# A gated delta recurrence with one head-shared kernel on one core: leaf solutions computed in contiguous rows and copied back by ScalarE

## The reference

```python
def step(S, t):
    q_t, k_t, v_t, a_t, b_t = t
    y = jnp.einsum('bhvk,bhk->bhv', S, k_t)
    err = y - v_t
    S = a_t[..., None] * S - (b_t[..., None] * err)[..., None] * k_t[:, :, None, :]
    o = jnp.einsum('bhvk,bhk->bhv', S, q_t)
    return (S, o)
```

## Time and profile before

| what | value |
|---|---|
| three runs | 3316.79, 3305.04, 3324.02 us; median 3316.79 |
| the profiled execution | 3323.35 us, its span 3321.6 us |
| mean granted TensorE clock | 0.968 |
| PE, PEld busy | 2941.5 us (89%), 2047.0 us (62%) |
| DVE busy | 2412.1 us (73%) |
| ACT, POOL busy | 1604.8 us (48%), 1287.5 us (39%) |

### The profile page before, as it was taken

How to read it: one execution, slowest core, us unless ns; L and a number is a source line. 1 busy time by engine, 2 the same in 40 slices (tenths; PEclk the granted TensorE clock), 3 DMA queues, 4 the chain that set the end, 5 groups by cost and what they waited for, 6 DMA issues and landing times. The chain is left out here.

```text
span 3321.6 us, 47953 instructions
## 1 busy us (share of the span) xinstructions
PE 2941.5 (89%) x14232; PEld 2047.0 (62%) x14232; DVE 2412.1 (73%) x4820; ACT 1604.8 (48%) x3480; POOL 1287.5 (39%) x1455
## 2 busy tenths in 40 slices
...
DMA packets 429785, 253.02 MB, mean 76 GB/s; under 512 B 400016, under 2 KB 412016, under 8 KB 414832
## 3 DMA queue, kind: packets, MB, share of 16 engines
...
## 5 line engine op out<-in xcount | busy, mean ns | idle before, releaser
L245 DVE SCALAR_TENSOR_TENSOR A_acc<-A_psY,A_w,A_acc 128x410 f32<-128x410 f32 (+1 forms) x720 | 419.3, 637 | 156.0 <-ACT A_acc L285 156.0
L771 POOL TENSOR_TENSOR B_WT<-B_WT,B_G 128x128 f32<-128x128 f32 (+2 forms) x224 | 191.4, 854 | 779.2 <-issue 448.8
L1072 ACT ACTIVATE B_WL<-B_psT 128x128 f32<-128x128 f32 (+2 forms) x480 | 150.0, 313 | 530.6 <-PE B_psT L1489 530.6
L345 PE MATMUL A_psY<-A_xT,A_w 128*128 128x413 f32 (+1 forms) x960 | 347.2, 510 | 9.0 <-PE A_psAG L351 7.7
L202 POOL TENSOR_TENSOR A_outs<-A_outs,A_acc 128x410 f32<-128x410 f32 (+1 forms) x240 | 229.2, 986 | 254.0 <-ACT A_outs L293 254.0
L345 PEld LDWEIGHTS A_psY<-A_xT,A_w 128*128 128x128 f32 x960 | 180.2, 189 | 165.5 <-issue 164.2
L986 DVE TENSOR_TENSOR B_NC<-B_NC,B_psM 128x256 f32<-128x256 f32 x480 | 198.8, 414 | 113.6 <-PE B_psM L1516 94.7
L989 DVE TENSOR_REDUCE B_W<-B_NC 128x64 f32<-128x320 f32 x512 | 248.8, 486 | 17.6
L1516 PE MATMUL B_psM<-B_BD,B_WL 128*128 128x128 f32 x1536 | 238.1, 297 | 9.1
L285 ACT ACTIVATE A_acc<-A_psY,A_w 128x410 f32<-128x410 f32 (+1 forms) x240 | 166.0, 692 | 163.1 <-PE A_psY L345 161.5
L1516 PEld LDWEIGHTS B_psM<-B_BD,B_WL 128*128 128x128 f32 x1536 | 196.7, 198 | 75.4 <-ACT B_WL L1072 74.7
...
## 6 DMA issues: line engine op xcount, KB each, us to landing
...
```

Of the source, the lines that this page charges most:

```text
L245: nc.vector.scalar_tensor_tensor(a, y, w[:, s, col:col + 1], a, ALU.mult, ALU.add)\
L345: last = nc.tensor.matmul(psY[p][:, y0:y0 + HALO + t1 - t0], wp[:, p, kt, :], xT[:, kt, t0:t1 + HALO], start=kt == 0, stop=kt == KT - 1)
L771: tt(dst, dst, gr, ALU.mult).then_inc(wsc.sem, 1)
L1072: copy = lambda out, in_: nc.scalar.activation(out, in_, ACT.Copy)
```

## The change

The solution is now worked out in `WTOK` (8 rows of 128 contiguous elements, otherwise used only between the end of a chunk's leaves and its state update), in `TMP` with its dimensions exchanged, and in `X`; ScalarE's new `solution_copy(i, n)`, n = 0, 1, 2, copies the finished coefficient rows to `NC`. L986 of leaves 0 and 8 waits for the last of these copies (`ncc`, 3) in place of the eighth step. `leaf_diagonals` has nine copies in place of five. The eight steps keep their number, their element counts and their place. One of the two state decays of leaf 10 moves to leaf 11, behind `row_pairs`. On TensorE the last job of leaf 14 waits for L986 of leaf 15, and the two copies into `WTOK` at the end of a chunk wait for `ncc` of the next chunk's first half.

```diff
-        TMP = sb("TMP", [128, HJ2, 4])
+        TMP = sb("TMP", [128, 4, HJ2])
...
-        gb, nc0 = Count(sem("block_decays"), 3), Count(sem("leaf_diagonals"), 5)
+        gb, nc0 = Count(sem("block_decays"), 3), Count(sem("leaf_diagonals"), 9)
...
-        ncs = Count(sem("leaf_solutions"), NCS)
+        ncs, ncc = Count(sem("leaf_solutions"), NCS), Count(sem("leaf_solutions_copied"), 3)
...
                 ps = rows(take_bank(dve, g if h else g - 1, "kk", h, 0))
-                tt(n[:, :, :, :, 11], ps[:, 1], a[:, 1], ALU.mult).then_inc(nl.sem, 1)
-                tt(n[:, :, :, :, 16], ps[:, 2], rr, ALU.mult).then_inc(nl.sem, 1)
+                wait(dve, ncc, i, 0)
+                tt(as_rows(WTOK[:])[:, 4], ps[:, 1], a[:, 1], ALU.mult).then_inc(nl.sem, 1)
+                tt(as_rows(WTOK[:])[:, 1], ps[:, 2], rr, ALU.mult).then_inc(nl.sem, 1)
...
-                step(1, 0, TMP[:, :, 0:3], n[:, :, 6:17:5], many(n[:, :, 0:1], 3), ALU.mult)
-                step(2, 0, n[:, :, 12:18:5], x02, many(n[:, :, 7:8], 2), ALU.mult)
-                step(3, 1, n[:, :, 5:16:5], n[:, :, 5:16:5], TMP[:, :, 0:3], ALU.add)
-                step(4, 0, n[:, :, 18:19], x2, n[:, :, 13:14], ALU.mult)
-                step(5, 3, tmp2, many(x02.unsqueeze(3), 2, 2), many(n[:, :, 5:7].unsqueeze(2), 2, 2), ALU.mult)
+                step(1, 0, TMP[:, 0:3], S[:, 1:8:3], many(TMP[:, 3:4], 3), ALU.mult)
+                step(2, 0, S[:, 2:6:3], x02, many(S[:, 5:6], 2), ALU.mult)
+                step(3, 1, S[:, 0:7:3], S[:, 0:7:3], TMP[:, 0:3], ALU.add)
+                step(4, 0, n[:, :, 18], X[:, 2], n[:, :, 13], ALU.mult)
+                step(5, 3, tmp2, many(x02.unsqueeze(2), 2, 2), many(S[:, 6:8].unsqueeze(1), 2, 2), ALU.mult)
                 step(6, 5, rows23, rows23, tmp2, ALU.add)
-                step(7, 6, TMP[:, :, 0:3], many(x2, 3), n[:, :, 10:13], ALU.mult)
-                step(8, 7, n[:, :, 15:18], n[:, :, 15:18], TMP[:, :, 0:3], ALU.add)
+                step(7, 6, TMP[:, 0:3], many(x2, 3), S[:, 3:6], ALU.mult)
+                step(8, 7, S[:, 0:3], S[:, 0:3], TMP[:, 0:3], ALU.add)
...
                     if j == 0 or j == 8:
-                        wait(dve, ncs, 2 * g + h, NCS)
+                        wait(dve, ncc, 2 * g + h, 3)
...
                         decay_state(g, 0)
-                        decay_state(g, 1)
                     elif j == 11 and more:
                         row_pairs(nxt)
+                        decay_state(g, 1)
                         leaf_solution(nxt, 1, 2)
...
                 for l in range(2):
                     copy(n[:, l, :, :, 7::6], f[:, l]).then_inc(nc0.sem, 1)
-                    copy(n[:, l, :, :, 0::5], v[:, l]).then_inc(nc0.sem, 1)
+                copy(n[:, :, :, :, 0], v[:, 0]).then_inc(nc0.sem, 1)
+                S = as_rows(WTOK[:])
+                if i:
+                    wait(act, stu, (i - 1) // 2, 0)
+                wait(act, ncs, i, 0)
+                wait(act, ncc, i, 0)
+                for k in range(3):
+                    copy(S[:, 6 - 3 * k], v[:, 1 + k]).then_inc(nc0.sem, 1)
+                copy(as_rows(TMP[:])[:, 3], v[:, 0]).then_inc(nc0.sem, 1)
+                copy(S[:, 5], f[:, :, :, :, 0]).then_inc(nc0.sem, 1)
+
+            def solution_copy(i, n):
+
+                flat = NC[:, i % 2].rearrange("p l h n c -> p c (l h n)")
+                wait(act, ncs, i, (3, 6, 8)[n])
+                w_ = 3 if n else 2
+                copy(flat[:, 5 * n + 5:5 * n + 5 + w_], WTOK[:, 6 - 3 * n:6 - 3 * n + w_]).then_inc(ncc.sem, 1)
...
                     elif j == 7 and more:
+                        solution_copy(2 * g + 1, 1)
+                        solution_copy(2 * g + 1, 2)
                         decay_copies(g + 1)
                         leaf_keys(2 * g + 2)
...
+                    elif j == 13 and more:
+                        solution_copy(2 * g + 2, 0)
                     elif j == 14:
                         if more:
+                            solution_copy(2 * g + 2, 1)
                             block_keys(2 * g + 2)
+                    elif j == 15 and more:
+                        solution_copy(2 * g + 2, 2)
...
                     for job in leaf_jobs(g, j):
+                        if j == 14 and job == leaf_jobs(g, j)[-1]:
+                            wait(pe, ap, g, J)
```

More of the change, by code:

```diff
@@ L643, in _ @@
                 if g + 1 < NCH:
-                    wait(sp, nc0, 2 * g + 1, 5)
+                    wait(sp, nc0, 2 * g + 1, 9)
                     load("C0", n, at)
@@ L828, in decays @@
                 wait(dve, gb, g - 2, 1)
-                wait(dve, nc0, 2 * g - 3, 5)
+                wait(dve, nc0, 2 * g - 3, 9)
                 a, e = by_leaf_row(A[:, s]), E[:, s]
@@ L1027, in chunk @@
                         decay_state(g, 0)
-                        decay_state(g, 1)
                     elif j == 11 and more:
                         row_pairs(nxt)
+                        decay_state(g, 1)
                         leaf_solution(nxt, 1, 2)
+                    elif j == 11:
+                        decay_state(g, 1)
                     elif j == 12 and more:
```

31 lines of the change are left out of this document (21 added, 10 removed).

## The result

The changed kernel takes 3334.72 us (median of 20 runs, 3326.55 to 3339.71); the kernel before, in 20 runs beside it, 3322.61 us (3305.04 to 3331.77). The medians lie 12.1 us apart. The ratio is 1.0041, 95% interval 1.0029 to 1.0054: slower by 13.6 us, where +33 was forecast. The direction held, the size did not. That 3334.72 stands inside the forecast's own range, 3333 to 3367, is luck: the kernel before came out at 3322.61 in these runs, 5.8 us above the 3316.79 that the forecast was added to. The profiled execution spans 3332.8 us (before 3321.6) at a mean granted clock of 0.967 (0.968).

A forecast was written before the change was run, and what follows sets the result against it. TensorE and VectorE were near full, VectorE deciding from leaf 6 to 8, with ScalarE's copies put behind it. Terms 20 + 12 - 10 + 11 = +33 us, carried to the median 3316.79, gave 3350 us; range 3333 to 3367, chance 0.50.

The forecast's parts named there:

- VectorE's prices: Solution steps: 384 contiguous elements take 546 ns, saving 1.8 us a solution, 115 us of VectorE's time in 64 solutions.
- ScalarE's price: Solution copies into NC: 384 elements at the 80-byte pitch take 0.90 us, between 0.50 and 1.05.
- The rival that ScalarE decides nothing: Copies run at contiguous pace, 384 in 0.50 us: -16 us, 3301, chance 0.12; 3275 if step 7 escapes GpSimd, 0.08.
- Leaf 7 to 8: L986 of leaf 8 waits for ScalarE's solution copy: loss 0.70 us (bounds: gain 0.5, loss 0.95).
- The rival that L771 misses step 7: At leaf 7 GpSimd's instruction misses step 7: leaf 8 costs -0.10 us, leaf 9 0; +3 us, 3320, chance 0.13.
- Leaf 4 to 7: Leaf 6 starts 0.45 us later behind leaf_diagonals' nine copies; steps 1 to 3 then gain 0.68 from leaf 6 to 7.
- T6 comes 0.45 us later: T6 is the start of L986 of leaf 6; nine ScalarE copies delay it 0.45 us (bounds 0 and 0.8).
- Leaf 8 to 9: ScalarE's queue behind the solution copies ends later than L947's start: loss 0.15 us (0 to 0.4).
- Leaf 10 to 12: The moved decay's 0.60 us is lost again and 0.64 more, in 19 chunks at full clock: +12 us.
- Leaf 12 to 15: Shorter steps gain 0.2 us at leaf 12 in 19 chunks, 0.4 at leaves 13 and 14 in 16: -10 us.
- Chunk's end: Last solution copy ahead of the WE copy costs 0.67 us in 16 even chunks, +11 us; odd ones covered.
- The clock rival: TensorE's clock, fallen to 0.50 about leaf 11 in 13 of 32 chunks, falls in all: +54 us, 3371, chance 0.17.

The follow-up runs named there:

- experiment 7: Changed kernel with solution copies of 2 in place of 128 elements a row, most of the solution not reaching NC; ratio to the kernel before 0.9978.
- experiment 5: Changed kernel with GpSimd's L771 after leaf 7 on 128 of its 512 elements; ratio to the kernel before 1.0004, leaf 7 to 8 from 5.99 to 5.26 us.
- Experiment 4: Kernel before with four more 128-element ScalarE copies in leaf_diagonals, into WTOK, which nobody reads; ratio to the kernel before 1.0095.
- experiment 6: Kernel before with one state decay moved from leaf 10 to 11, ratio 1.0021; changed kernel with that decay put back, 1.0067.
- experiment 9: Changed kernel, four edits: step 8 into NC at leaf 7, last copy late, TensorE's wait out, value copies earlier: 1.001; with leaf 9's decay transposes doubled 0.9905.
- experiments 2 and 3: Changed kernel with the chunk's last solution copy behind the WE copy, ratio 1.0048; the same without TensorE's new wait at leaf 14's last job, 1.0006.
- experiment 8: TensorE's eight decay transposes of leaf 9 issued twice: ratio to the kernel before 0.9985 in the changed kernel, 0.9938 in the kernel before.
- experiments 1 to 3: Changed kernel with step 8 writing NC itself, third copy gone, 1.0038; with the chunk's last copy behind WE's, 1.0048; that without TensorE's new wait, 1.0006.

## Why the prediction was right, and where it failed

- **VectorE's prices**: 546 ns for 384 contiguous elements is right, 553 measured. The 115 us saved are not: the groups show 62. Step 2 lost 0.19 us and not 0.43, since its 840 ns were the mean of 0.61 at leaf 6 and 1.08 at leaf 12 and the second stayed long (0.89); step 7 lost 0.03 at leaf 7 and 0.05 at leaf 14 and not 0.47; step 1 lost 0.21 and not 0.30. The sum of the forecast did not use this figure.
- **ScalarE's price** (0.90 for 384 at the 80-byte pitch): right in kind, 1.00 measured. The rule of the Trainium skill, page "ScalarE: Activation LUTs", section "What ACT_TABLE_LOAD costs", gives a time by the number of elements alone, an estimate of 0.51 for 384. "Whatever the pattern" was the prediction's reading of it; the page does not speak of the pitch. At this pitch the measurement decides against the rule. The rival that ScalarE decides nothing fell with that price; with copies of 0.21 us (experiment 7) the change is faster, as that rival had it, but by 7 us and not 16, with the nine copies of leaf_diagonals still in place.
- **Leaf 7 to 8**: right. +0.79 for +0.70; the 0.09 is the copy's 1.00 in place of 0.90. That GpSimd holds step 7 is shown by experiment 5: a quarter of the elements, -0.73 us. The faster steps 4 to 6 moved the end of step 7 by 0.2 (T7 + 4.33 for 4.53) and not its length (1.40 for 1.43). The rival that L771 misses step 7 fell. Both ends, 0.42 and 0.41 us behind GpSimd's, agree with the exclusive lock that the Trainium skill describes in "SBUF — State Buffer", section "SBUF: two separate sides".
- **Leaf 4 to 7: the step that failed.** The forecast took the later start of leaf 6 (+0.45) as paid in full, beside the steps' 0.68. The start moved by 0.22: L852 starts 0.63 us later in the leaf and not 1.0, because the nine copies take 2.68 us (forecast 2.9) and the pairs copies, now contiguous, are 0.15 shorter, which was counted at leaf 12 and not here. And those 0.22 were not paid. VectorE's scale of leaf 6 (L991, after L993) ends just behind GpSimd's two L761, started by leaf 5. In the chunk of the earlier trace rows, where T5 is 1803.52, the kernel before shows:

```profile
1806.61 2.06 POOL L761 TENSOR_TENSOR B_PQ<-B_PQ,B_G 128x512 f32<-128x512 f32 x2
...
1807.93 0.87 DVE L991 TENSOR_TENSOR B_WT<-B_W,B_E 128x64 f32<-128x64 f32 x1
```

The scale ended at T5 + 5.28 before and at T5 + 5.27 after (2515.50 + 0.66 - 2510.89), though leaf 6 began later. It took 0.87 us before, 0.66 after, 0.27 with GpSimd out of the way. So T5 to T7 fell by 0.67, the steps' gain alone, where -0.23 had been forecast: 0.44 x 32 = 14 us of the 20 that are missing from +33. Experiment 4 has it from the other side (+0.67 at leaf 6, +0.07 at leaf 7). The prediction looked for GpSimd's hold only in step 7. The step that failed is thus its "T6 comes 0.45 us later", added in full to the sum.
- **Leaf 8 to 9**: +0.15 forecast, 0 measured at either length. The rest copy starts 1.33 us after L988, but L949 keeps its 1.95: 5 us too many. That the long length stood in six chunks fewer, 3 us, was not forecast.
- **Leaf 10 to 12**: the decay's 0.60 leaves leaf 10 as said. Leaf 12 then came 0.36 later in sum and not 0.64 (for which the prediction's own terms, 1.0 less 0.3, would have given 0.7): from leaf 10's copy of ones to the end of the nine copies it took 0.65 us more and not 1.0, and from there to the copy into WE 0.29 less. In the 12 half-clock chunks, leaf 10 to 12 took 8.42 us for 8.41 before, so there the delay is covered, as said. At full clock a delay of ScalarE is paid in full here, as experiment 4 shows (3.25 to 4.23). The decay itself costs nothing (experiment 6), and moving the value copies gave 0.46 back (experiment 9).
- **Leaf 12 to 15**: -8.3 us for -10. **Chunk's end**: right for even chunks, 0.66 for 0.67, and 0.09 in odd ones. But "nothing" for TensorE's new wait is not so in general: with the copy moved, the wait holds the even end at 11.05 where it is 10.68 without it (experiments 2 and 3).
- **The clock rival.** It was given +21 us over the forecast if all chunks fell; they did not, 12 fell for 13. That the clock is nonetheless a larger item than the whole change is shown: 18 and 23 us went with it in the two kernels (experiment 8) and 35 in the one with four edits. What decides which chunks fall stays open. Filling 1.03 us of TensorE's idle time in leaf 9 took the fall at leaf 11 away in all three kernels tried, but kernels with the same times from leaf 9 to 11 (the changed one and experiments 1 to 3) had 6 to 17 such chunks.
- **All terms together**, on the two profiled executions (+33 forecast, +11.2 measured): leaves 4 to 7 came out 14 us lower than forecast, leaf 8 to 9 8 us, leaf 10 to 12 with the clock 4 or 5, the first and last chunks 4; leaf 7 to 8 came out 3 us higher, leaf 12 to 15 with the chunk's end 3, and the start of the recurrence 2.5.
